# Two column one-hots of four edge columns each in place of one of eight, in the placement of an edge sort

## The reference

```python
edge_index = jnp.stack([src, dst])                     # 100000 edges, 6250 nodes, 256 features
x = x + gnn(layernorm(x), W1, b1, W2, b2, edge_index)
x = x + ffn(layernorm(x), Wg, bg, W1, b1, W2, b2)      # 8 experts, top 2

def gnn(x, W1, b1, W2, b2, edge_index):
    dst, nbr = edge_index
    agg = segment_sum(x[nbr], dst); cnt = segment_sum(ones, dst)
    return x @ W1.T + b1 + (agg / maximum(cnt, 1)[:, None]) @ W2.T + b2

def ffn(x, ...):                                       # softmax over the 2 best of 8 gates
    return sum(combine[:, e] * (relu(x @ W1[e].T + b1[e]) @ W2[e].T + b2[e]) for e in range(8))
```

## Time and profile before

| what | value |
|---|---|
| median of three runs | 1956.68 us |
| span of the profiled execution (first to last instruction; no other time of it is given) | 1953.6 us |
| TensorE busy, matmuls | 1762.7 us (90%) |
| GpSimd busy | 1194.5 us (61%) |
| ScalarE busy | 1118.8 us (57%) |
| VectorE busy | 967.4 us (50%) |
| line 650, gathers | 784, from 108.6 to 1147.7 us, 801.5 us busy |
| line 1473, column one-hots | 100, from 69.2 to 802.7 us, 102.2 us busy |

### The profile page before, as it was taken

One profiled execution on the slowest core, in us unless ns is written; L12 is line 12 of the kernel. 1 busy time (PEld: TensorE's weight loads), 2 busy tenths in 40 slices (PEclk: granted clock), 3 DMA queues, 4 the chain that ended last, 5 costly groups with the idle time before them and its releaser, 6 DMA issues.

```text
span 1953.6 us, 41490 instructions
## 1 busy us (share of the span) xinstructions
PE 1762.7 (90%) x11167; PEld 1488.9 (76%) x11167; DVE 967.4 (50%) x2315; ACT 1118.8 (57%) x3316; POOL 1194.5 (61%) x1141
## 2 busy tenths in 40 slices
PE   6888998899887888878887889999999999999997
PEld 4655875588555677656665768999999999999997
DVE  6868977898467887633334786311111111111111
ACT  5964875477544699765652667544444444444443
POOL 1167777778777777777777753454454455444543
PEclk9989999999999999999999999999999999999999
DMA  9323333333333333344543777724424424242421
GB/s 313 102 87 103 94 97 103 103 88 87 100 103 106 100 97 96 100 128 138 143 138 110 236 243 242 216 40 124 127 44 117 102 60 123 38 126 38 124 36 20
DMA packets 113112, 224.31 MB, mean 115 GB/s; under 512 B 27286, under 2 KB 76604, under 8 KB 107094
## 3 DMA queue, kind: packets, MB, share of 16 engines
q0 software_dynamic: 61152, 129.45, 26.6%
q1 hardware_dynamic: 32576, 74.98, 11.3%
q10 hardware_dynamic: 19254, 18.32, 3.0%
HBM read 371.77 MB, written 34.91 MB: 208 GB/s over the span
## 4 chain that ended last, share of the span: by engine, by line
PE 45%; POOL 30%; issue 11%; DMA 6%; DVE 4%; ACT 1%; SPq 1%; DVEq 0%; POOLq 0%; ACTq 0%
POOL arena L650 30%; PE bank L1315 19%; PE bank L1331 18%; DMA arena<-ytab,arena 4%; PE bank L1280 2%; PE bank L1055 2%; PE bank L1303 1%; PE bank L1101 1%; DVE agg L1949 1%; DMA gw<-in_gw2t 1%; SPq L465 1%; DMA ytab<-arena 1%; DMA agg<-in_b 0%; ACT arena L738 0%; ACT arena L753 0%
## 5 line engine op out<-in xcount | busy, mean ns | idle before, releaser
L650 POOL DMA_INDIRECT arena<-ytab,arena x784 | 801.5, 1022 | 240.1 <-issue 228.9
L1280 PE MATMUL bank<-arena 128*128 x2356 | 627.5, 393 | 121.3 <-SPq L525 120.5
L1280 PEld LDWEIGHTS bank<-arena 128*128 128x128 f32 x2356 | 412.4, 195 | 221.4 <-issue 160.7
L948 ACT ACTIVATE arena<-bank,agg 128x128 f32<-128x128 f32 x840 | 308.7, 368 | 400.4 <-PE bank L1315 343.0
L1315 PEld LDWEIGHTS bank<-arena,agg 128*128 128x128 f32 x3360 | 392.2, 192 | 5.6 <-issue 0.7
L1315 PE MATMUL bank<-arena,agg 128*128 128x128 f32 x3360 | 393.8, 276 | 0.3 <-issue 0.3
L1949 DVE TENSOR_TENSOR agg<-agg,bank 128x257 f32 x589 | 247.8, 421 | 292.8 <-PE bank L1280 252.7
L1331 PE MATMUL bank<-agg,arena 128*128 128x256 f32 x1680 | 380.1, 379 | 0.3 <-DMA agg<-in_b 0.3
L683 POOL DMA_INDIRECT out<-arena x105 | 171.0, 1629 | 323.6 <-issue 229.3
L1331 PEld LDWEIGHTS bank<-agg,arena 128*128 128x128 f32 x1680 | 311.0, 190 | 38.5 <-DMA agg<-in_b 0.6
L794 ACT ACTIVATE arena<-lanes,arena 128x128 f16<-128x128 f16 x816 | 247.9, 386 | 21.2 <-DVEq L1577 21.2
(11 more groups left out here) (275 smaller groups left out, 1655.3 us busy)
## 6 DMA issues: line engine op xcount, KB each, us to landing
agg<-in_w SPq DMA_DIRECT2D x210, 1024.0 KB
agg<-in_b SPq DMA_DIRECT2D x105, 128.0 KB
arena<-ytab,arena POOLq DMA_INDIRECT x784
ytab<-arena SPq DMA_DIRECT2D x12, 512.0 KB, 3.2
arena<-in_xt ACTq DMA_DIRECT2D x24, 256.0 KB, 2.9
node<-in_x SPq DMA_DIRECT2D x6, 896.0 KB, 12.3
agg<-in_xt SPq DMA_DIRECT2D x6, 896.0 KB, 12.9
out<-node ACTq DMA_DIRECT2D x6, 896.0 KB
```

The costliest lines, as they stand in the source:

```text
L650: pool.indirect_dma_start(out=rows[:, v % RU, h, 0:D], out_offset=None, in_=ytab[:, :], in_offset=bass.IndirectOffsetOnAxis(ap=rowidx[g % ...
L948: act.activation(hT[:, m, :], hidden_bank(j, m)[:, 0:T], ACT.Relu, bias=b1b[:, b, m:m + 1]).then_inc(s_fr, 1)
L1280: mm = pe.matmul(bank[bank_of(n)][:, 0:W], onehot[n // QUAD % 2][:, n % QUAD, h, :], pair[:, h * W:(h + 1) * W], start=(h == 0), stop=(h = ...
```

## The change

The column one-hot of a tile is written by two instructions of four edge columns each, and each of them raises `s_c`. TensorE waits for the first of them ahead of column 0 and for the second ahead of column 4 (`PC // 2`). `positions`, which waits for all column one-hots of the groups before, counts in two.

```diff
                 if u == 0:
-                    pe.wait_ge(s_c, j + 1)
+                    pe.wait_ge(s_c, 2 * j + 1)
                     pe.wait_ge(s_vd, j + 1)
+                if u == PC // 2:
+                    pe.wait_ge(s_c, 2 * j + 2)
...
-                v.wait_ge(s_c, PT0[s])
+                v.wait_ge(s_c, 2 * PT0[s])
...
-                v.tensor_tensor(in_pairs(ohc[j % PB][0:EP, :, 0:CH[s]]), counted(PC, CH[s]), pairs(pos_cq[0:EP, 0, c:c + PC, :], PC, CH[s]),
-                                ALU.is_equal).then_inc(s_c, 1)
+                for a in range(0, PC, PC // 2):
+                    b = a + PC // 2
+                    v.tensor_tensor(in_pairs(ohc[j % PB][0:EP, a:b, 0:CH[s]]), counted(PC // 2, CH[s]), pairs(pos_cq[0:EP, 0, c + a:c + b, :], PC // 2, CH[s]),
+                                    ALU.is_equal).then_inc(s_c, 1)
```

## The result

The changed kernel takes 1944.55 us (median of six runs, 1942.45 to 1950.18) where the kernel before takes 1957.22 (six runs, 1956.52 to 1960.34): a ratio of 0.9934, 95% interval 0.9922 to 0.9947. The span of the profiled execution went from 1953.6 to 1941.4 us.

The account below looks back on a forecast made before the run. The prediction took GpSimd's gathers to set the pace through most of the sort. A gain of 14.0 us less 1.0 at the start made 13.0, so 1943.7 us; likeliest range 1938 to 1950, 8-in-10 range 1937 to 1950.

Parts of the forecast that it names:

- What bounds the kernel: Through most of the sort GpSimd's gathers (line 650) set the pace: 68.3% of the chain of 250 to 1100 us.
- The start: First group's placement, before any gather: 16 added VectorE instructions at 0.06 us each cost 1.0 us, bounds 0 to 1.0.
- Line 1473's hold: Gathers held by the column one-hot's instruction in the three later placements: the sum falls from 27.2 to 12.1 us.
- the common phase: Group of 240 columns: 9 gathers stand still about 0.42 us into line 1473; with halves 0.22 us of hold are left.
- Given back to other lines: Gathers that come earlier meet other VectorE instructions later, so the gain in the three placements is 14 us.
- the stepped 16: Gain from stepping all gathers along VectorE's rows: 47 us lost with line 1473 whole, 31 with halves; scaled to 14.
- The gain reaches the end: From the gathers to the program's end: GpSimd doesn't run out of free rows or lists, so the whole 14 us count.
- the rival of the held-back gain: TensorE can't follow, GpSimd waits for buffers or lists; only the last stretch's gain less the start: 1953.2 us, chance 0.07.
- The rival that the pair holds GpSimd: Two halves leave no gap for a gather and hold it as one instruction did: 1957.7 us, chance 0.05.
- no gather of 1.9 us would be left: Sign in the trace after: beside a column one-hot no gather takes 1.9 us any more.
- VectorE as the pace: Rival: TensorE waits at line 1055 for VectorE, 100 tiles at 0.06 us cost 6.0 us: 1962.7 us, chance 0.05.
- The sum: Whole kernel: 14.0 us from the gathers less 1.0 at the start, 13.0 us faster; 1943.7 us, chance 0.83.

Follow-up runs that it names:

- quarters: Column one-hots of all groups in four instructions of two columns each, one signal, against the kernel before: 1941.97 us, ratio 0.9907.
- seven columns and one: Column one-hots in two instructions, of seven columns and of one, with one signal, against the kernel before: 1962.47 us, ratio 1.0009.
- the lanes in halves: One-hots of the lanes (line 1661) in two halves, column one-hots whole, against the kernel before: 1954.76 us, ratio 0.9979.
- quarters in the later groups: Column one-hots in quarters in the second to fourth group, whole in the first, one signal, against the kernel before: 1937.70 us, ratio 0.9894.
- both in halves: Column one-hots in halves in the second to fourth group, and the lanes' one-hots in halves, against the kernel before: 1945.66 us, ratio 0.9933.
- both in quarters: Column one-hots in quarters in the second to fourth group, and the lanes' one-hots in quarters, against the kernel before: 1938.05 us, ratio 0.9900.

## Why the prediction was right, step by step

- *What bounds the kernel* held: GpSimd's gathers, in the trace before and after, and a change to VectorE alone moved the time through them.
- *The start*, 1.0 us: the first gather came at 109.55 in place of 108.57. Right, and 2.9 us with quarters as well.
- *Line 1473's hold*, 27.2 to 12.1 us: it came to 10.4, over 48 gathers in place of 45. In the group of 240 columns nine of the 16 gathers that met a half were held 0.20 to 0.24 us, as the 0.22 that I left to the common phase there. In that of 256 the phase of 0.20 us, with its 0.48 left, came once; most stood still about 0.48 us into a half and were held about 0.2.
- *Given back to other lines*, taken as 43 / 47 of the stepped 16: line 1486 went from 5.2 to 8.8 us, line 1472 from 9.3 to 6.2. In the three placements the gain was 14.1 us against 14, but that match is in part luck: the rows of a stretch, mine before too, count a gather that its border cuts as a whole one. With every gather put whole into the stretch where it starts, the placements lost 44.5 us before and 29.2 after, a gain of 15.3. All gathers gained 801.5 - 785.4 = 16.1. The rest is a sum of opposite signs in stretches where I had forecast about 0: 1.6 us more lost between the first two placements, 2.0 less behind the last.
- *The gain reaches the end*: not all of it, and the step that I left out is the landing of the rows. These are pieces of the chain of waits (start, length), before and then after:

```profile
1106.85 5.35 DMA arena<-ytab,arena
1112.37 1.37 PE bank L1280 x4
```

```profile
1093.21 7.00 DMA arena<-ytab,arena
1100.38 2.08 PE bank L1282 x4
```

  The gather that starts there is the 754th in both traces and the last in the chain; behind it TensorE and VectorE set the pace, and the 15 us of the last gather count for nothing. The 754th came 13.6 us earlier, its rows took 1.65 us longer to land, and TensorE, which waited for them, went on 12.0 us earlier, as did the experts. In the seven other traces whose chain leaves the gathers at this one, the kernel before among them, the landing took 5.24 to 5.52 us; it was 5.32 in the kernel with the same halves and one signal. So the 7.00 belongs to this execution and isn't shown to come of the change; its cause stays open. One gather waited 0.64 us longer than the usual 0.30 for a buffer (1121.22), which is the rival of the held-back gain, but by then the gathers were out of the chain. Over the traces the time from the last gather to the end lies between 804 and 810 us, without an order that I could name.
- *The rival that the pair holds GpSimd* was refuted as a rule, but it happens: once in some 150 held gathers after the change, three times with seven columns and one, twice with the lanes in halves and with quarters in the later groups, four times with both in halves and five with both in quarters. In the other traces no gather beside a column one-hot missed its turn. My sentence that no gather of 1.9 us would be left beside a column one-hot was wrong by that one (2.04 us). What makes a gather miss its turn stays open. That the hold is one of the SBUF operands' ports I take from the earlier trace rows and from the Trainium skill, SBUF — State Buffer, "Who interferes with whom"; beside lines 1482 and 1949, which read one tensor from SBUF, no gather was lengthened in the trace before (22 and 180 met them). Nearest to a test there is a pair of lines with the same operation on 128 x 256 elements: line 1681, with one operand in PSUM, lengthened none of 18 gathers, and line 1702, with both in SBUF (it also sums its row), 6 of 12. A kernel in which the same line reads one operand from elsewhere wasn't built, so the ports are argued and not shown.
- *VectorE as the pace* was refuted: with 300 added instructions in place of 100 the kernel got no slower (0.9907 against 0.9934).

The sum, 13.0 us, came out at 12.7 by the medians and 12.2 by the profiled spans. The mechanism held, and so nearly did the size: GpSimd was 13.6 us ahead at the last gather that counts. That the end comes as near as this owes something to luck, since a gain somewhat above the 14 and a late landing that I had no term for stand against each other.

## What to carry to other kernels

Where GpSimd's indirect DMAs set the pace, look at the spread of their durations, and lay VectorE's rows beside the long ones: a VectorE instruction with two SBUF operands can be costly for its length alone, though VectorE is far from the bound. Cut the longest of them, where VectorE has time to spare, and expect others to hold part of what is set free. A gain stepped on the old rows can be off by several us either way (here 7 forecast and 3.6 found, none forecast and 4.4 found, in the gathers' busy time). And what the gathers gain counts up to the last of them that stands in the chain of waits.

## What was not expected of the hardware

A gather that is held by a row of such instructions nearly always goes on between two of them, though the second already stands in the trace as running (0.09 us of overlap). Now and then it doesn't, and is held to the end of the row (2.88 us in place of 0.95 at the most); what decides this is open. And the sum of the holds repeats between executions though the single holds don't: 784 gathers were busy 801.5 and 801.4 us in two traces of the same kernel, 790.6 and 790.2 in those of another, with only 94 of some 165 held gathers in common there.
